# Layer statistics of twelve tiles taken among the expert units, and settled in two parts

## The reference

```
x = x + L0_attn(layernorm(x), ...)          # attention, 16 heads of 128, 4-bit weights
x = x + L0_xattn(layernorm(x), ctx, ...)    # attention over context and x
x = x + L0_ffn(layernorm(x), ...)           # gated FFN, 2 of 4 kept
x = x + L1_attn(layernorm(x), ...)          # attention with ALiBi
x = x + L1_xattn(layernorm(x), ctx)         # channel attention, no weights
x = x + L1_ffn(layernorm(x), ...)           # 32 experts, top 8, rerouted

def _layernorm(x, axis=-1, eps=1e-05):
    m = jnp.mean(x, axis=axis, keepdims=True)
    v = jnp.var(x, axis=axis, keepdims=True)
    return (x - m) / jnp.sqrt(v + eps)
```

## Time and profile before

| | |
|---|---|
| median of 3 runs | 1916.67 us (1914.07 to 1920.19) |
| profiled execution, its own time | 1911.81 us |
| its span | 1910.0 us |
| PE busy | 1707.1 us (89%) |
| DVE busy | 1489.9 us (78%) |
| ACT busy | 1031.2 us (54%) |
| POOL busy | 720.3 us (38%) |
| mean granted TensorE clock | 0.975 |

### The profile page before, as it was taken

The page is one execution under the profiler, slowest core; times in us unless marked ns, Lnnn a source line. Parts: engine busy times, 40 slices in busy tenths (PEclk is TensorE's granted clock), DMA queues, the critical chain, the costliest instruction groups (busy, mean ns, idle before and its releaser), DMA issues.

```text
span 1910.0 us, 43448 instructions
## 1 busy us (share of the span) xinstructions
PE 1707.1 (89%) x15840; PEld 1004.0 (53%) x15840; DVE 1489.9 (78%) x2884; ACT 1031.2 (54%) x2056; POOL 720.3 (38%) x965
## 2 busy tenths in 40 slices
PE   5999999689999999979977996777777889999998
PEld 2656665347777777755544551222222356656555
DVE  6866666579989899857886889999999478676654
ACT  3665655345555555534436765888888533323222
POOL 4635321387677677612345453444531000000000
PEclk9999999889999999989989997999999999999999
DMA  9601110000000000000001211333321023222121
GB/s 254 177 24 51 29 41 2 17 23 12 10 13 14 7 10 4 2 9 1 1 1 36 59 38 52 94 91 96 96 72 41 17 76 96 88 63 72 63 83 50
DMA packets 87662, 94.92 MB, mean 50 GB/s; under 512 B 17568, under 2 KB 63264, under 8 KB 87456
## 3 DMA queue, kind: packets, MB, share of 16 engines
q1 hardware_dynamic: 83712, 87.76, 16.3%
q10 hardware_dynamic: 2976, 2.32, 0.5%
q0 software_dynamic: 768, 2.10, 0.4%
HBM read 78.51 MB, written 10.22 MB: 46 GB/s over the span
## 4 chain that ended last, share of the span: by engine, by line
DVE 23%; PE 22%; issue 6%; POOL 3%; ACT 1%; DVEq 0%; POOLq 0%; ACTq 0%
PE ps L275 18%; DVE arena L1592 14%; POOL arena L1147 2%; PE ps L1859 1%; PE ps L1502 1%; PE ps L1856 1%; DVE arena L2440 1%; DVE arena L2436 0%; DVE arena L1201 0%; DVE arena L244 0%; POOL arena L2013 0%; DVE arena L2371 0%; DVE arena L2369 0%; DVE arena L1952 0%; ACT arena L2312 0%
## 5 line engine op out<-in xcount | busy, mean ns | idle before, releaser
L275 PE MATMUL ps<-arena 128*128 128x512 f16 (+6 forms) x6464 | 1090.9, 324 | 54.6 <-POOL arena L1147 9.6
L275 PEld LDWEIGHTS ps<-arena 128*128 128x128 f16 (+1 forms) x6464 | 602.1, 99 | 442.0 <-issue 37.8
L1578 ACT ACTIVATE arena<-ps 128x512 f32<-128x512 f32 x512 | 278.6, 598 | 71.1 <-PE ps L1510 48.5
L1592 DVE TENSOR_REDUCE arena<-ps 128x4 f32<-128x1024 f32 x256 | 305.3, 1218 | 10.8 <-PE ps L1502 10.5
L1502 PE MATMUL ps<-arena 31*128 31x256 f16 x1024 | 102.2, 275 | 72.7 <-ACT arena L1578 52.1
L1558 PE MATMUL ps<-arena 128*32 128x256 f32 x2048 | 164.1, 392 | 2.7 <-ACT arena L1587 0.6
L2430 DVE TENSOR_TENSOR arena<-ps,arena 128x512 f32<-128x512 f32 x96 | 66.1, 688 | 126.8 <-ACT arena L2322 111.6
L2322 ACT ACTIVATE arena<-ps 128x512 f32<-128x512 f32 x96 | 57.1, 596 | 176.9 <-PE ps L275 176.4
L1502 PEld LDWEIGHTS ps<-arena 31*128 31x128 f16 x1024 | 34.8, 92 | 187.6 <-DVE arena L1592 151.0
L1051 POOL TENSOR_TENSOR arena<-arena 128x512 f32<-128x512 f32 x96 | 98.8, 1043 | 45.1 <-DVE arena L221 44.0
L652 POOL TENSOR_TENSOR arena<-arena 128x256 f32<-128x256 f32 x64 | 39.5, 617 | 180.4 <-DVE arena L617 180.4
(11 more groups left out here) (203 smaller groups left out, 2931.1 us busy)
## 6 DMA issues: line engine op xcount, KB each, us to landing
arena<-moe_cw SPq DMA_DIRECT2D x64, 192.0 KB, 2.8
arena<-moe_cw SPq DMA_DIRECT2D x64, 128.0 KB, 2.9
arena<-in_L_ffn_gate_up_proj SPq DMA_DIRECT2D x16, 384.0 KB, 3.4
ch_out<-arena SPq DMA_DIRECT2D x32, 128.0 KB
arena<-moe_cw SPq DMA_DIRECT2D x64, 64.0 KB, 2.7
ch_keys<-arena SPq DMA_DIRECT2D x48, 64.0 KB, 2.0
arena<-ch_keys SPq DMA_DIRECT2D x64, 48.0 KB
arena<-arena SPq DMA_DIRECT2D x192, 16.0 KB
```

Source lines behind the costliest of these rows:

```text
L275: last = nc.tensor.matmul(out, a, b, start=start and n == 0, stop=stop and n == len(pairs) - 1, skip_group_check=not group)
L1578: nc.scalar.activation(pT[:, b % 3, g], ps[:, T[n % len(T)], :].rearrange("p (u t) -> p u t", u=KD), ACT.Exp, scale=CH_SCALE).then_inc(s_e ...
L1592: nc.vector.tensor_reduce(m[:, half % 2, 2 * half_pair:2 * half_pair + 2, j, :], ps[:, bank(user):bank(user) + 2, :].rearrange("p g (u s) ...
```

## The change

DVE measures only tiles 0 to 3 in the channel attention and settles only these four behind it. Tiles 4 to 12 are measured among units 3 to 7 of the experts, and tiles 4 to 11 are settled there, at unit 6, by a settling of its own (`moe_middle`). Tiles 13 to 15 and their settling keep their units. The work on other engines and all transfers keep their order.

```
@@ vector_step @@
-        if pair == 1 and t % CH_SETS == 3 and tile >= 3:
+        if pair == 1 and t % CH_SETS == 3 and 3 <= tile < 3 + SUBS:
             measured(dve, tile - 3)
@@ vector @@
-        settle(core, dve, "moe_first", 4, range(TILES - SUBS))
-
-    def vector_rest(dve, k):
-
-        if k < 2:
-            invert(dve, TILES - 2 + k)
-        else:
-            measured(dve, TILES - 5 + k)
-        if k == 4:
+        settle(core, dve, "moe_first", 4, range(SUBS))
+
+    def vector_rest(dve, inverts, measures):
+
+        for tile in inverts:
+            invert(dve, tile)
+        for tile in measures:
+            measured(dve, tile)
+        if TILES - SUBS - 1 in measures:
+            settle(core, dve, "moe_middle", 4, range(SUBS, TILES - SUBS))
+        if TILES - 1 in measures:
             settle(core, dve, "moe_last", 4, range(TILES - SUBS, TILES))
@@ the table @@
-MOE_CHANNEL_REST = (2, 8, 9, 12, 13)
+MOE_CHANNEL_REST = {2: ((14,), ()), 3: ((), (4, 5)), 4: ((), (6, 7)), 5: ((), (8, 9)), 6: ((), (10, 11)), 7: ((), (12,)),
+                    8: ((15,), ()), 9: ((), (13,)), 12: ((), (14,)), 13: ((), (15,))}
@@ the experts' vector program @@
             if n in MOE_CHANNEL_REST:
-                channel().rest(dve, MOE_CHANNEL_REST.index(n))
+                channel().rest(dve, *MOE_CHANNEL_REST[n])
```

## The result

| | before | after |
|---|---|---|
| median of 20 runs each | 1913.18 us | 1919.58 us |
| profiled execution, its own time | 1911.81 us | 1924.73 us |
| its span | 1910.0 us | 1922.9 us |
| its mean granted clock | 0.975 | 0.970 |

The ratio is 1.0027, with a 95% interval of 1.0016 to 1.0038: 5.2 us more (3.1 to 7.3), within the 0.3% called the same. It is not the ratio of the medians, which lie 6.4 us apart; it is close to that of the means (1919.33 and 1914.18 us). The forecast was 1918.4 us, 1.7 us above a median that more runs put at 1913.18. So the time fell inside the range, but the difference is three times the one forecast. One of the 20 runs after took 4240.9 us and is left out of the ratio.

What follows compares the result with a forecast made beforehand. It took an ACT-PE loop to pace the channel attention, partly DVE, and DVE's router chain to bound the experts' start. Saving 2.7 and adding 4.4 us to 1916.67 gave 1918.4 us, range 1912.5 to 1922.1.

Steps and rivals of the forecast that it cites:

- Within 0.3% and somewhat slower: Whole kernel: a difference within 0.3% (5.75 us), chance 0.89 for the same, with the likeliest time 1.7 us slower.
- The sum: Whole kernel: 2.7 us saved against 4.4 us added, +1.7 us (+0.7 to +2.4).
- Taken out of the channel attention ... 2.2 us: Channel attention: nine of thirteen BN_STATS removed, each at 0.25 us, save 2.2 us.
- What is left is the pace of the early tiles: Channel attention: late tiles would then run at the early tiles' pace, 20.42 us in place of 20.66.
- the pace doesn't come: Rival: another chain (POOL, SP's transfers) holds late tiles at 20.66 us; only 0.5 saved, +3.9, 1920.6 us; chance 0.08.
- The settling behind it ... 0.5 us: Settling behind the channel attention: four aggregates in place of twelve save 0.5 us (0.3 to 0.7).
- Added among units 3 to 6 ... Added in unit 7: Experts' start: moved statistics and middle settling delay the router's end by 4.4 us (3.6 to 4.9).
- PE's wait ahead of L2207: Sign in the changed trace: this wait of PE would be between 0 and 0.4 us.
- The end of the router's last operation: Sign in the changed trace: DVE's last router operation would end 1.7 us later than 1536.87.
- The clock rivals: PE's half clock behind the coefficients' turn: one stretch more 1920.1 us (0.15), one less 1916.7 (0.08), three stretches 1923.5 (0.05).

Runs made afterwards that it cites:

- after_again: The changed kernel run once more without an edit, beside the kernel before; ratio 1.0034.
- left_out: Kernel before with the nine BN_STATS and the aggregates of tiles 4 to 11 left out altogether, using an earlier stage's statistics; ratio 1.0012.
- unit0: Changed kernel with the nine statistics and the middle settling moved to unit 0, where DVE waits for ACT; ratio 1.0012.
- warm: Changed kernel with 14 more matmuls, into a bank nobody reads, ahead of the turn of step 0's coefficients; ratio 1.0030.
- unit0_fix: unit0 with the transfer of a tile's first turned maxima (L1434) and the experts' constants moved earlier in SyncE's order; ratio 0.9978.
- before_again: The kernel before without an edit, run as a kernel of its own against before; ratio 1.0007.
- best_fix: unit0_fix with statistics of tiles 0 to 3 made seven maxima ahead of L1616, and tiles 13 and 15 moved to units 0 and 6; ratio 0.9979.
- added_only: Kernel before with statistics of tiles 4 to 12 made a second time among units 3 to 7 and a second settling at unit 6; ratio 1.0048.
- added_again: The kernel added_only run once more against before; ratio 1.0046.
- the three kernels of the first move: Changed kernel, unit0, and unit0 with further statistics moves, each with L1434 moved ahead of load_total and five L1423, constants unmoved; ratios 1.0022, 0.9994, 0.9985.

## Why the prediction was right or wrong

*Within 0.3% and somewhat slower* was right. The sum, +1.7 us, was too low: the interval is +3.1 to +7.3. That the time itself, 1918.4 us for 1919.58, was nearly met is luck: the median of three runs it stands on was 3.5 us too high, and the sum too low by about as much.

*"Taken out of the channel attention ... 2.2 us"* is the step that failed. The single half did shorten as it says, from 10.46 to 10.21 us, with ACT's pause at 0.59 where it had been 0.83. But five executions with this channel attention (changed, after_again, left_out, unit0, warm) took 297.85 to 300.25 us for the halves, 299.46 in the mean, and the four with that of before 299.46, 299.44, 299.72 and 300.86, or 299.87. Of 2.2 us, 0.4 was kept in the mean; single traces scatter by 1 us around it. With it falls *"What is left is the pace of the early tiles"*: the early tiles don't show the late tiles' queue. In tile 2 of the kernel before, from which the 10.21 us was read, SyncE issued L1434 0.62 us after the maxima were there; in tiles 3 to 12 it was 2.5 to 3.1 us. The rival *the pace doesn't come* named the right engine and got 0.08, though the late tiles are not held at an even 20.66 us: most halves run at 10.21, and single ones stop for the transfer, up to 12.63. Its argument against itself, a half of tile 2 at 10.21 us, was the weak point. unit0_fix shows the cause by taking it away: with the transfer in time, the 2.2 us came, and 0.9 more, which are the two halves of the kernel before that were late for the same transfer (tile 10 with 10.35 us and tile 11 with 10.97).

*"The settling behind it ... 0.5 us"* is mis-sized: 0.33, near its lower bound of 0.3, for the reason given there. A later small operation met POOL, and now even two did, 0.25 us on L215 and 0.41 on L217, each ending within 0.02 us of a POOL operation. By the rule of the Trainium skill, "SBUF — State Buffer", section "SBUF: two separate sides", that one of the two engines holds the shared ports for a whole instruction, this is what should come of it, and the trace agrees.

*"Added among units 3 to 6 ... Added in unit 7"*, 4.4 us, was nearly right: PE's waits before the turn grew by 6.33 - 2.21 = 4.1 us, the router's part by 4.9, at the upper bound (4.5 against before_again). The middle settling took 3.09 us for a forecast of 3.1. Above the sum are two meetings with POOL: a pause of 0.50 us on DVE's chain of small operations at 1517.07, while L1685 ran, and L2393, the router's weighing, at 1.64 us beside L1685 and L1687, for 1.22 before.

*PE's wait ahead of L2207*, now L2210, was 0.35 us, inside 0 to 0.4. *The end of the router's last operation* came 8.5 us later, not 1.7; of these, 3.9 had already been lost up to the settling, to half clock before the stage among them.

*The clock rivals.* Half clock behind the turn went on for 6.82 us in place of 3.4, and two later stretches came in the profiled execution, so its view fitted the rivals. Over the runs they don't stand: the total half clock doesn't go with the waits, and warm, which filled the wait, won nothing. The Trainium skill, "TensorE: Matmul & The Clock Gate", section "What's actually happening", has it that activity is what releases the clock. That agrees with the one place in warm, and it doesn't predict which execution throttles where.

*The sum in its new form:* -0.4 for the channel attention, -0.3 for the settling, +4.9 for the router makes +4.2 us, inside the measured interval. With the 0.7 us that the first half loses by the moved transfer, the same arithmetic gives -3.1 + 0.7 - 0.4 = -2.8 us (0.9985) for unit0_fix and -4.1 + 0.7 - 0.4 - 0.9 = -4.7 (0.9975) for best_fix, where the last term is its router's part, 50.74 for 51.6 at full clock; both lie inside their intervals.

*Left open.* The 3 to 4 us of added_only and added_again beyond the 4.9. And the stretch ahead of the channel attention, whose code no edit touched: it took 146.8 to 147.1 us in seven of the profiled executions (before, before_again, those with the work at unit 0) and 148.5 to 149.9 in the other seven (those with work in units 3 to 7, and left_out). Taken from the start of the execution, the first maximum came at 1141.0 to 1145.3 us in the former seven and at 1145.4 to 1151.1 in the latter, 4.2 us later in the mean, which is as much as the whole sum in its new form. The code is laid out differently behind it, but no run tried that. If the medians hold such an offset, it would account for what added_only, added_again and left_out are above their parts, and the fit of +4.2 us with the changed kernel would be partly luck. unit0_fix and best_fix are on the side of before, so their gain doesn't rest on it.

## What to carry to other kernels

Before you credit a saving in a paced loop, take every transfer that the loop needs once in a round and read its slack: from the data being ready, through what stands ahead of it in its queue, to the reader. If the slack is smaller than the saving, the saving moves the stop and no more; here 0 to 0.5 us of slack faced 0.25 us a tile, and one transfer that took 0.9 us longer than usual used it up without any change. When you move the transfer, look at what it pushes back: here the totals and the weights that POOL splits. Then give the moved work to a wait that is long for another reason: here DVE's 10 us behind ACT at unit 0, and not a stretch whose end PE waits for.

## What was not expected of the hardware

Where PE waited for L1434, it mostly went on 1.8 to 1.9 us behind its issue, but 2.74 us in tile 11 of before, 3.00 in one tile of added_again and 3.4 to 3.6 in tile 3 of the three kernels of the first move. Each issue at this place held SyncE's queue for 0.5 to 0.7 us, so a position behind six others is worth some 4 us. The fourteen traces, of the same or nearly the same program, have 93 to 121 us at half clock, and whole runs of one kernel moved with it: 0.976 and 1914.83 us, 0.970 and 1924.73. A difference of 5 us could be read only from some ten runs of each kernel and, in a single trace, only from parts with equal clock.
